# A 16-pair software pipeline: VectorE's second norm ahead of its fourth add, TensorE's value products ahead of its fourth score group

## The reference

```
x   = emb[tok]*sqrt(128) + pos;  q = x@Wq+bq;  k = x@Wk+bk;  v = x@Wv+bv
s[i,j] = sum_d attn_scale[d] * tanh(q[i,d] + k[j,d])        # additive attention
x1  = layernorm(x + softmax(s)@v@Wo + bo)
x2  = layernorm(x1 + relu(x1@W1+bf1)@W2 + bf2)              # "second norm"
h0  = x2;  xa = layernorm(h0)
h1  = h0 + causal_attention(xa; 8 heads of width 128)@Wo
out = h1 + moe(layernorm(h1); 64 experts, top 2, and a shared branch) + a last feed-forward
```

## Time and profile before

| | |
|---|---|
| median of 3 runs | 1176.58 us (1172.55 to 1179.44) |
| the profiled execution | 1169.94 us, span 1168.1 us |
| busy in the span | PE 872.7 us (75%), PEld 665.8 (57%), DVE 708.7 (61%), ACT 667.8 (57%), POOL 392.2 (34%) |
| stretch from 214.2 to 255.2 us, one turn | PE 34.13 us, DVE 35.91, ACT 31.62, POOL 10.76 busy |
| granted TensorE clock | 0.909 of full speed over the span |

### The profile page before, as it was taken

One profiled execution on the slowest core, in us unless ns is written; L12 is line 12 of the kernel. 1 busy time (PEld: TensorE's weight loads), 2 busy tenths in 40 slices (PEclk: granted clock), 3 DMA queues, 4 the chain that ended last, 5 costly groups with the idle time before them and its releaser, 6 DMA issues.

```text
span 1168.1 us, 24664 instructions
## 1 busy us (share of the span) xinstructions
PE 872.7 (75%) x7427; PEld 665.8 (57%) x7427; DVE 708.7 (61%) x2209; ACT 667.8 (57%) x1643; POOL 392.2 (34%) x458
## 2 busy tenths in 40 slices
PE   3457889789778978987898887167766666665887
PEld 1235566556555655655665565166656656665787
DVE  4398878988898898889889643311211112123776
ACT  3266878777777877777787554033433434342343
POOL 7500111322331232233123333365655555551111
PEclk9978899999999999999998888578998998897999
DMA  8200000000000000000000000447766675665000
GB/s 196 29 1 1 1 8 2 8 8 0 7 7 7 0 7 7 0 7 7 7 0 8 8 8 8 90 131 212 210 183 193 182 196 169 179 185 112 14 17 21
DMA packets 53976, 71.08 MB, mean 61 GB/s; under 512 B 10818, under 2 KB 40624, under 8 KB 53936
## 3 DMA queue, kind: packets, MB, share of 16 engines
q1 hardware_dynamic: 45456, 62.56, 19.7%
q0 software_dynamic: 8480, 8.01, 3.0%
HBM read 64.17 MB, written 11.03 MB: 64 GB/s over the span
## 4 chain that ended last, share of the span: by engine, by line
PE 36%; issue 25%; DVE 19%; DMA 8%; another core or an unknown queue 5%; POOL 3%; SPq 2%; ACT 1%; DVEq 0%; POOLq 0%
PE b_s L1207 6%; DMA b2buf<-in_L_ffn_b 5%; PE big L1334 5%; PE b_o L1374 5%; DVE tbuf L794 5%; PE big L1486 4%; PE big L1324 4%; DVE spread L794 4%; POOL pr L424 2%; DVE pr L921 2%; PE b_qk L1501 2%; PE b_s L1501 2%; PE big L1361 1%; SPq L343 1%
## 5 line engine op out<-in xcount | busy, mean ns | idle before, releaser
L1486 PE MATMUL big<-hbT,wbuf 128*128 128x128 f32 x672 | 108.5, 312 | 91.7 <-DMA b2buf<-in_L_ffn_b 47.4
L794 DVE TENSOR_TENSOR tbuf<-qT,b_qk 128x2304 f32<-128x2304 f32 x64 | 162.7, 2547 | 19.6 <-remote 10.7
L657 ACT ACTIVATE act_h<-big,wbuf 128x128 f32<-128x128 f32 x336 | 95.7, 368 | 122.5 <-PE big L1486 75.7
L541 ACT ACTIVATE tbuf<-tbuf 128x2304 f32<-128x2304 f32 x64 | 135.6, 2119 | 46.6 <-DVE tbuf L794 38.4
L1486 PEld LDWEIGHTS big<-hbT,wbuf 128*128 128x128 f32 x672 | 94.0, 216 | 103.8 <-issue 50.7
L1207 PE MATMUL b_s<-tbuf,apad 128*32 128x192 f32 x1536 | 97.5, 393 | 59.4 <-ACT p L550 51.8
L1092 DVE TENSOR_SCALAR hbT<-b_t,cols 128x128 f32<-128x128 f32 x84 | 34.3, 409 | 147.8 <-PE b_t L1479 85.1
L482 POOL DMA_INDIRECT hrow<-tok_dram,igather x84 | 85.5, 1018 | 80.9 <-PE b_t L1479 37.4
L491 POOL DMA_INDIRECT eo_dram<-eo,iscatter x84 | 85.9, 1023 | 56.7 <-issue 32.7
L424 POOL TENSOR_TENSOR pr<-pr,rs 96x384 f32<-96x384 f32 x64 | 52.7, 824 | 149.5 <-DVE rs L928 149.5
L1207 PEld LDWEIGHTS b_s<-tbuf,apad 128*32 128x32 f32 x1536 | 51.0, 126 | 90.4 <-issue 48.8
(11 more groups left out here) (209 smaller groups left out, 1916.0 us busy)
## 6 DMA issues: line engine op xcount, KB each, us to landing
wbuf<-in_wpack SPq DMA_DIRECT2D x84, 514.0 KB
b2buf<-in_L_ffn_b SPq DMA_DIRECT2D x84, 64.0 KB
tok_dram<-tn SPq DMA_DIRECT2D x32, 96.0 KB
spread<-eo_dram SPq DMA_DIRECT2D x1, 2688.0 KB, 16.0
out<-of SPq DMA_DIRECT2D x16, 96.0 KB, 1.7
hrow<-tok_dram,igather POOLq DMA_INDIRECT x84
eo_dram<-eo,iscatter POOLq DMA_INDIRECT x84
tab_dram<-tid_now,slot_now POOLq DMA_INDIRECT x64
```

The source lines that it names most:

```text
L541: act.activation(v, v, ACT.Tanh).then_inc(s["tanh"], 1)
L657: last = act.activation(act_h[:, r % 2, c * TILE:(c + 1) * TILE], big[r % 2][:, c * TILE:(c + 1) * TILE], ACT.Silu, bias=wbuf[:, r, 2 * DF ...
L794: dve.tensor_tensor(ring[c % TRING].rearrange("p (x m n) -> p x m n", m=CQ, n=N), qv.unsqueeze(3).to_broadcast([D, SPLIT * QG, CQ, N]), kv ...
L1486: last = pe.matmul(big[r % 2][:, c * TILE:(c + 1) * TILE], wbuf[:, r, c * D:(c + 1) * D], hbT[:, r % 2, :], start=True, stop=True)
```

## The change

Only the order of the lists changes. No stage is added or removed, and no wait is edited.

- DVE: `x2_norm` and `inv_sums` 2 go ahead of `add` 3 (they stood behind `add` 3 and `p1T_copy`).
- ACT: `x1T_affine` goes ahead of `tanh` 6 (it stood right behind it).
- PE: `attend2` 1 goes ahead of `score` 2, and `xa_turn` behind it. `score` 3 goes behind `v_rows`, `xs_turn`, `heads_g` 2 and 3, `attend2` 2, `heads_v` 0 and `heads_v` 1. `attend2` 2 goes ahead of `heads_v` 0. `heads_v` 1 goes ahead of `score` 3, `x1_turn` and `score` 4.

```diff
@@ ACT
+                at(n, 1, x1T_affine)
                 at(n, 0, tanh, 6)
-                at(n, 1, x1T_affine)
@@ DVE
+                at(n, 2, x2_norm)
+                at(n, 3, inv_sums, 2)
                 at(n, 0, add, 3)
                 at(n, 1, p1T_copy)
-                at(n, 2, x2_norm)
-                at(n, 3, inv_sums, 2)
@@ PE
                 at(n, 3, attend2, 0)
+                at(n, 3, attend2, 1)
+                at(n, 0, score, 2)
                 at(n, 2, xa_turn)
-                at(n, 0, score, 2)
                 at(n, 3, pr_turn, 3)
                 at(n, 2, heads_g, 0)
                 at(n, 2, heads_g, 1)
-                at(n, 3, attend2, 1)
-                at(n, 0, score, 3)
                 at(n, 0, v_rows)
                 at(n, -1, xs_turn)
                 at(n, 2, heads_g, 2)
                 at(n, 2, heads_g, 3)
+                at(n, 3, attend2, 2)
                 at(n, 2, heads_v, 0)
-                at(n, 3, attend2, 2)
+                at(n, 2, heads_v, 1)
+                at(n, 0, score, 3)
                 at(n, 1, x1_turn)
                 at(n, 0, score, 4)
-                at(n, 2, heads_v, 1)
                 at(n, 2, heads_v, 2)
```

## The result

The changed kernel takes 1186.57 us (median of 8 runs, 1185.85 to 1192.11), the kernel before on the same chip 1177.91 us (8 runs, 1172.55 to 1181.27): a ratio of 1.0075, with an interval of 1.0055 to 1.0095. The change makes the kernel 8.7 us slower; 7.6 us faster was forecast, with 1180 us as the upper end. The profiled execution took 1190.51 us, its span is 1188.7 us.

What follows compares the result with a forecast made beforehand. PE was taken to set the turn's end from `heads_g` 0 to `qk`, DVE the rest. 12 turns x 0.95 = 11.4 us, less 1.0, 0.8 and 2.0, gave 7.6: from 1176.6 to 1169.0 us; range 1164 less 2, to 1180.

Steps and rivals of the forecast that it cites:

- What bounds the kernel: PE sets the turn's end from `heads_g` 0 up to `qk`, DVE the rest; a full turn takes 40.9 us.
- the one from `xa_turn` to `xaT_copy`: ACT's copy behind PE's transpose: `xa_turn` at 431.25, `xaT_copy` at 431.6, so `heads_g` 0 comes 0.1 us earlier.
- The cover: Ahead of `heads_g` 0: if the moved `attend2` 1 took longer there, `heads_g` 0 would be late by all of it.
- the wait of `v_rows`: PE's `v_rows`, moved up by 2 us, meets DVE's x1 rows: 0.1 us of wait, ends zero and 0.5.
- The steps ahead of `add` 3: On DVE, `x2_norm` and `inv_sums` 2 take 1.75 us, so `add` 3 ends 1.75 us later.
- DVE loses nothing: On DVE, `add` 4 starts at 425.77 as before, although `x2_norm` and `inv_sums` 2 move ahead of `add` 3.
- `score` 3 and `add` 7: PE's `score` 3 ends at 439.3; DVE's `add` 7 loses 0.3 us, covered at `mask_max` 0 with 0.7 to spare.
- `tanh` 6: On ACT, behind `x1T_affine`, it starts at 440.5 instead of 439.22; `vv_copy` 1 keeps 0.5 us of cover before `ffn1` 0.
- Turn 0: `xs_turn` ahead of `score` 3 waits for DVE's rows, PE arriving about 1 us early: -1.0 us.
- The tail: Turns 16 and 17: `attend2` 1, moved beside `attend2` 0 at the lower clock, pays once: -0.8 us.
- The clock: PE's low-clock stretch may lie elsewhere in the turn or last longer: 0.17 us a turn, -2.0 us in all.
- Slower: Low clock over `attend2` 0 and 1 ahead of `heads_g` 0: turn 0.8 us longer, 1188 us; chance 0.13.

Runs made afterwards that it cites:

- Run 13: Only the change's PE and ACT part, DVE's list as before, `xa_turn` ahead of `score` 2, against the kernel before: ratio 0.9932.
- run 10: The changed kernel with `xa_turn` put back ahead of `score` 2, on a third chip: ratio 0.9983 to the kernel before.
- run 12: Only the change's PE and ACT part, DVE's list as before, `xa_turn` ahead of `score` 2, on a third chip: ratio 0.9927 to the kernel before.
- run 2: The changed kernel with `scatter_ids` 1 moved on POOL right behind `scatter_ids` 0, late in the turn: 1180.35 us, ratio 1.0066 to the kernel before.
- run 1: The changed kernel with `xa_turn` put back ahead of `score` 2: 1171.96 us, ratio 0.9996 to the kernel before.
- run 9: The changed kernel, unedited, timed again on a third chip: ratio 0.9997 to the kernel before.
- run 16: The changed kernel with `scatter_ids` 1 moved behind `keep_x` on POOL, on a fourth chip: turns of 40.65 to 40.94 us.
- runs 1 to 4 and 13 to 16: The changed kernel with one line moved, or parts of the change alone, on chips where PE's completions can be late: ratios from 0.9932 to 1.0066 among those given.
- runs 5 to 12: The kernel before, the changed kernel and variants of it, on chips where no PE completion was late in that stretch; the kernel before took 1112.24 us on one.

## Why the prediction was wrong

**What bounds the kernel: right.** PE sets the turn from `heads_g` 0 to `qk`, and in the kernel before what moves `heads_g` 0 moves the turn. With the new list it does so only when it is later than `v_rows`' wait for `x1_rows`. Run 13's turn, 0.77 us shorter than before, comes from PE's and ACT's order alone.

**The step that failed is the one from `xa_turn` to `xaT_copy`.** The prediction had "`xa_turn` comes at 431.25", 12.5 after the maximum, and "`xaT_copy` starts at 431.6", 12.85. `xa_turn` came at 12.97, and `xaT_copy` at 14.66. The first half, 0.5 us, is DVE's (below), the second 1.35: I took the time from one group's matmuls to the next engine's start as nothing where the order on PE had changed, and on this chip it is over a microsecond beside the scatter DMAs of `scatter_ids` 1. The cover was called thin for a longer `attend2` 1; what ate it was a delay that stood in the profile before, on `pr_turn` 3, whose `prT_copy` 3 started at 432.78 after a wait of 0.75 us although the matmuls had ended at 431.43. I read that wait as unimportant, which it was there, and didn't ask why it was so long.

**DVE: a size was off, and with it the wait of `v_rows`.** The steps ahead of `add` 3 were put at 1.75 us and took 432.35 - 430.06 = 2.29: `x2_norm` 1.15 instead of 0.60. Then `attend1` is 1.1 us late, not 0.63, and "DVE loses nothing" is wrong: the same instructions cost it 0.55 us a turn, and `x1_rows` ends that much later. The sum had a wait of `v_rows` for "DVE's x1 rows", put at 0.1 us; it is 0.13 with DVE's list as it was, and 0.52 more with the change. Runs 10 and 12 give the price with no hold: 40.65 against 40.13 a turn, 0.9983 against 0.9927. `normalise` 2 did come 2.15 us earlier, at 5.56 instead of 7.71, and `pr_turn` 2 no longer waits for it; it starts at 8.79 all the same, 0.1 us later than before, since `attend1` is late.

The 1.15 us beside POOL's `normalise` 1 fit a rule of the Trainium skill ("SBUF — State Buffer", section "Who interferes with whom"): a VectorE instruction with two SBUF inputs contends with a GpSimd instruction that reads SBUF. Here these are `xg` with the beta row on one side and a product of two tiles on the other. The trace agrees, with 1.15 against 0.60 us, and it is VectorE that pays: `normalise` 1 takes 0.84 us beside it and 0.82 alone. The single records tell more: the row of the pair that starts just behind `normalise` 1 (at 2.72) is the slow one, the second in the profile after (0.32, then 0.91 us) and the first in run 2 (0.88, then 0.34), where the pair begins at 2.81. So the engines do not hold each other up through semaphores alone, as was said ahead of the prediction. No run here moved `normalise` 1 instead of `x2_norm`.

**The other steps.** `score` 3 and `add` 7: `add` 7 was to lose 0.3 us and started at 22.40, 2.05 later than before, because all of PE was late; its 0.7 us of cover at `mask_max` 0 was enough (0.67 us of wait left). `tanh` 6 came at 23.49 against the 21.75 worked out, late with the rest of PE, and PE had no wait for `vv_copy` 1. Turn 0 was put at -1.0: the first maximum comes at 72.27 instead of 70.85 us, 1.4 later. The distance behind it, turn 1, was put at nothing and is 0.85 longer. The tail was put at -0.8: from the last maximum to the table there is hardly a difference (85.4 us against 85.2), but turn 15, which was to gain 0.95, is 0.7 longer. Of the first turns not all is the change's own for certain: the first distance is 29.01 in run 1 and 26.53 in run 10, which is the same kernel. The clock was put at 2.0 us. Turn 10 after has it low for longer, in the stretches from the maximum on (columns as in rows 1):

```profile
427.50:431.00 3.50, 2.41 (x26) 1.26 (x26) 3.32 (x20) 3.12 (x12) 1.50 (x2) 0.50 0.01 0
431.00:434.80 3.80, 3.23 (x32) 1.61 (x30) 3.58 (x9) 3.31 (x11) 1.56 (x3) 0.69 0.00 0
434.80:438.00 3.20, 2.81 (x19) 2.06 (x20) 3.20 (x5) 2.78 (x3) 0.00 (x0) 1.00 0.00 0
```

That is 3.5 + 3.8 x 0.31/0.50 = 5.9 us at 1.2 GHz against 3.4 before, all ahead of `attend1`, where PE has waits. Where it lies later it can cost: run 9 has turns of 40.65 and, from the tenth on, of 40.83 to 40.93, the latter with `attend1` itself at the lower clock (1.09 us against 0.69) and `v_rows` at 15.66 to 15.76. In turn 10 of run 10, with `xa_turn` ahead of `score` 2, `attend1` is as slow and the turn is 40.65 all the same: `v_rows` still waits for DVE.

**The sum.** The turn of 40.90 loses 0.77 with PE's order and `xa_turn` ahead of `score` 2 (runs 12 and 13), gains 0.52 from DVE's part (run 10 against 12), and 1.05 from `xa_turn` behind `score` 2 in the hold (run 1 against after): 41.70, the measured turn. Terms from different chips can be added here, since run 1's kernel has the same 40.65 with and without the hold (run 10), and run 12's the same 40.13 (run 13). Without the hold the last term is 0 to 0.28, and the changed kernel is level with before (0.9997). The forecast's -0.95 had the first term, and none of the other two. Of the first, the 0.97 is 0.90 (when `v_rows` doesn't wait it is 26.57 us from `heads_g` 0 to the next maximum, against 27.47 before), the 0.1 of an earlier `heads_g` 0 did not come (13.44 in run 12, 13.43 before), and `v_rows`' wait is 0.13. Up to the table the profiles differ by 13.7 us and the medians of the whole by 8.7; what the experts give back or the execution profiled adds I can't say from one profile each, and run 2 shows the same in small.

**The rivals.** "Slower" came true by size (1188 was worked out, 1186.57 measured) and not by mechanism: the place, `xa_turn` behind both value products, is that of the rival, but the low clock was over by 434.8, ahead of them.

**The faster version** is the change's PE and ACT part with `xa_turn` ahead of `score` 2 and DVE's list as it was: 0.9932 (0.9903 to 0.9960) with the hold, 0.9911 and 0.9927 without.

## What to carry to other kernels

When a group of matmuls is moved, read not only where its rows end but when the next engine starts after them, and compare with other groups: a wait that outlasts its releaser by a microsecond marks a place in which nothing on the critical path may stand. When an instruction of VectorE is moved, look at what GpSimd runs at the new place; here that took two rows from 0.60 to 1.15 us, and the time was paid where another engine waited for a later step of VectorE's list. And try the parts of a change one by one and in the order that each would have alone: of these two, one gained 0.7% once a single line was put right, and the other cost 0.5%.

## What the runs showed of the hardware

On some chips PE's completions are signalled late beside GpSimd's indirect scatter DMAs. In turns 5 to 14 `score` 2 and `pr_turn` 3, which ended 0.6 to 2.6 us after the first DMA of `scatter_ids` 1 began, raised their semaphores 0.2 to 1.7 us after the last matmul (two records, of 4.8, aside), 2.0 to 3.0 us after that beginning, where the score groups elsewhere in the turn take 0.04 us. All eight profiles of the first result and of runs 1 to 4 and 13 to 16 that have those DMAs in that place show it, and none of the eight of runs 5 to 12. Moving the DMAs took it away (runs 2 and 16), but it doesn't come wherever such DMAs are: in run 16 groups that ended 1.6 to 2.8 us after the first DMA were in time, and in turn 15 of the same profile five groups 0.9 to 2.6 us after it were 0.3 to 1.9 us late. The chips with it are also those that feed the experts more slowly; whether the two have one cause stays open, and so does what holds the signal and what part the score groups have in it. The same program thus takes 1112 or 1173 us by the chip, and a change can be worth -0.03% on one and +0.75% on another.

VectorE's instruction with two SBUF inputs took 0.91 us instead of 0.34 when it started just behind the start of a 0.84 us GpSimd product, and the GpSimd instruction lost 0.02 us.
